# Projection stage of a two-layer attention kernel: where the squares and the normalising factors of q, k and v are computed

## Chip, cores and metric

The kernel runs on one core of a Trainium2 chip. The metric is the device time of one execution in microseconds, the median of several runs. The core has a matrix engine (TensorE, PE in the rows), a vector engine (VectorE, DVE), an activation engine (ScalarE, ACT), a general engine (GpSimd, POOL) and a queue engine (SyncE, SP). Each follows its own instruction list; they wait for one another only through semaphores.

## Reference

The part that the change touches is the front of the first layer's attention. With `hs` of 4 x 1024 tokens and 128 features, 16 heads of width 64:

```python
q = _silu(hs @ Wq + bq).reshape(Bn, Ln, H, DK).transpose(0, 2, 1, 3)
k = _silu(hs @ Wk + bk).reshape(Bn, Ln, H, DK).transpose(0, 2, 1, 3)
v = _silu(hs @ Wv + bv).reshape(Bn, Ln, H, DV).transpose(0, 2, 1, 3)
beta = jax.nn.sigmoid(hs @ Wb + bb).transpose(0, 2, 1)
...
q = q * jax.lax.rsqrt(jnp.sum(q * q, axis=-1, keepdims=True) + 1e-06)
k = k * jax.lax.rsqrt(jnp.sum(k * k, axis=-1, keepdims=True) + 1e-06)
...
g = (hs @ Wg + bg).reshape(Bn, Ln, H, DV)
```

The recurrence over tokens, a gated output projection, a quantised feed-forward block and a second layer (causal attention and eight experts) follow or precede; the change leaves them alone.

## The kernel before

The program is a row of phases. Each ends with `end_phase`, at which all five engines wait for one another, so nothing of the next phase starts before the slowest engine of this one is through. The change touches the projection phase alone.

In that phase the 4096 tokens are 32 tiles (`T`) of 128. For each tile TensorE fills eight PSUM banks of 512 columns (q, k, v and g, two banks each); a bank is one fp32 product (L1631, two recorded matmuls) and one bf16 product that adds the bias (L1632). Bank n of a tile waits for ACT's `Silu` of bank n of the tile before (`p_silu`). ACT turns the banks into `prj`, which holds four tiles (L1891), and waits before a tile until the store of the tile four earlier has landed (`p_stored`). GpSimd squares q, k and v, 1024 columns each, into `prj_sq`, which has one slot for each of the three (L1506); the slot must have been read by the reduction of the tile before (`p_red`). VectorE sums the squares by head (L2072) into `prj_n` for q and k and into `vv` for v. ACT takes the square root of the 32 sums of q and k (L1895). VectorE takes the reciprocal (L2077), copies the roots of beta, `sb_tok`, beside them as the factors of v (L2079), multiplies those of k by them (L2080), and scales the 3072 columns of q, k and v in place (L2082, `p_normed`). SP then stores the tile (L1379). VectorE does this with a lag of one tile: the three reductions of tile i, then the factors and the scaling of tile i-1. Each engine's order is the order in which the code is written; there is no scheduler.

After the last tile VectorE multiplies `vv` twice by `sb_tok` (L2084, L2085), TensorE turns it (L1637), ACT takes roots (L1899), SP stores them, and the phase ends. The next phase starts with loads of `ka` from the stored projections.

Of the kernel before, what the change touches and what calls it, by code (L numbers as in the profile page):

```python
# [10 lines left out]
ALU = mybir.AluOpType  # L11
ACT = mybir.ActivationFunctionType
AX = mybir.AxisListType.X
ds = bass.ds

P = 128
D = 128
B, L = 4, 1024
T = B * L // P
H0, DK = 16, 64  # L20
HD = H0 * DK
# [40 lines left out]
def layer_kernel(nc, a, out):  # L62

    ctx = ExitStack()
    with ctx:
        def sem(name):
            return ctx.enter_context(nc.semaphore(name))

        def sb(name, shape, dt=F32, scope=ctx):
            return scope.enter_context(nc.sbuf_tensor(name, shape, dt))  # L70
# [23 lines left out]
        bank = [banks[:, 512 * n:512 * n + 512] for n in range(8)]  # L94
# [35 lines left out]
        s2 = ExitStack()  # L130
# [8 lines left out]
        prj = sb("prj", [P, 4, 4 * HD], scope=s2)  # L139
        prj_sq = sb("prj_sq", [P, 3, HD], scope=s2)  # L140
        prj_n = sb("prj_n", [P, 2, 2, 2 * H0], scope=s2)
        prj_f = sb("prj_f", [P, 2, 3 * H0], scope=s2)
        prj_eps = sb("prj_eps", [P, 1], scope=s2)
        sbeta = sb("sbeta", [H0, B * L], scope=s2)
        sb_tok = sb("sb_tok", [P, T, H0], scope=s2)
        vv = sb("vv", [P, T, H0], scope=s2)
# [197 lines left out]
        p_sq = sem("p_sq")  # L344
        p_mm = sem("p_mm")
        p_silu = sem("p_silu")
        p_var = sem("p_var")
        p_std = sem("p_std")
        v_prj = sem("v_prj")
        p_normed = sem("p_normed")  # L350
        p_red = sem("p_red")
        p_stored = [sem(f"p_stored{n}") for n in range(2)] + [hq_done, h_turned]
        res_out, res_in = hT_done, down_done
        prj_sems = p_stored[2:4] + [res_out, res_in]
# [30 lines left out]
        sbt_set = sem("sbt_set")  # L385
# [67 lines left out]
        cleared = sem("cleared")  # L453
# [16 lines left out]
        def end_phase(eng):  # L470

            phases[eng] = phases.get(eng, 0) + 5
            eng.drain().then_inc(phase, 1)
            eng.wait_ge(phase, phases[eng])
# [79 lines left out]
        def prob_at(j):  # L554
            return sum(TB - x for x in range(j)) * P
# [927 lines left out]
        def _(pool):  # L1483
# [13 lines left out]

            for x in prj_sems:
                pool.sem_clear(x).then_inc(cleared, 1)
            for i in range(T):  # L1500
                for w in range(3):
                    pool.wait_ge(p_silu, 8 * i + 2 * w + 2)
                    if i:
                        pool.wait_ge(p_red, 3 * (i - 1) + w + 1)
                    x = prj[:, i % 4, HD * w:HD * w + HD]
                    pool.tensor_tensor(prj_sq[:, w, :], x, x, ALU.mult).then_inc(p_sq, 1)  # L1506
            end_phase(pool)
            chunk_pool(pool)
            with capped(pool):
# [321 lines left out]
        def _(act):  # L1831
# [50 lines left out]
            act.activation(sbeta[:, :], gates[0:H0, :], ACT.Sqrt).then_inc(sb_root, 1)  # L1882
            act.wait_ge(bias_set, 7)
            act.wait_ge(cleared, len(prj_sems))
            for i in range(T + 1):
                if i < T:
                    if i >= 4:
                        act.wait_ge(p_stored[i % 4], 16 * (i // 4))
                    for n in range(8):
                        act.wait_ge(p_mm, 8 * i + n + 1)  # L1890
                        act.activation(prj[:, i % 4, 512 * n:512 * n + 512], bank[n], ACT.Silu).then_inc(p_silu, 1)  # L1891
                if i >= 1:
                    y = (i - 1) % 2
                    act.wait_ge(p_red, 3 * (i - 1) + 2)
                    act.activation(prj_n[:, y, 1, :], prj_n[:, y, 0, :], ACT.Sqrt, bias=prj_eps[:, 0:1]).then_inc(p_std, 1)  # L1895
            act.wait_ge(g_stored, 16)
            for n in range(8):
                act.wait_ge(vv_turned, n + 1)
# [74 lines left out]
            for kind, s, k in program:  # L1973
                if kind == "b":
# [4 lines left out]
                    at, w = prob_at(j) + first - P * j, end - first  # L1979
# [14 lines left out]
        def _(dve):  # L1994
# [58 lines left out]
            bia = Count(dve, bias_set)  # L2053
            bia.n = 1
            bia.link(dve.memset(bias3[:, :], 0.0))
            bia.link(dve.memset(prj_eps[:, :], 1e-6))
            bia.link(dve.tensor_copy(bias_hi[:, :], raw3))
            bia.link(dve.scalar_tensor_tensor(out=rest3, in0=bias_hi[:, :], scalar=bias_part[:, 0:1], in1=raw3, op0=ALU.mult, op1=ALU.add))
            bia.link(dve.tensor_copy(bias_hi[:, :], rest3))
# [2 lines left out]
            dve.tensor_copy(sb_tok[:, :, :].rearrange("p t h -> p (t h)"), bank[0]).then_inc(sbt_set, 1)  # L2062
            dve.wait_ge(sbt_set, 1)
            prc = Count(dve, v_prj)
            for i in range(T + 1):
                if i < T:
                    y = i % 2
                    if i >= 2:
                        dve.wait_ge(p_std, i - 1)
                    for w, dst in ((0, prj_n[:, y, 0, 0:H0]), (1, prj_n[:, y, 0, H0:2 * H0]), (2, vv[:, i, :])):  # L2070
                        dve.wait_ge(p_sq, 3 * i + w + 1)
                        dve.tensor_reduce(dst, prj_sq[:, w, :].rearrange("p (h d) -> p h d", d=DK), AX, ALU.add).then_inc(p_red, 1)  # L2072
                if i >= 1:
                    t, y = i - 1, (i - 1) % 2
                    root = sb_tok[:, t, :]
                    dve.wait_ge(p_std, t + 1)
                    dve.reciprocal(prj_f[:, y, 0:2 * H0], prj_n[:, y, 1, :]).then_inc(v_prj, 1)  # L2077
                    prc.n += 1
                    prc.link(dve.tensor_copy(prj_f[:, y, 2 * H0:3 * H0], root))  # L2079
                    prc.link(dve.tensor_tensor(prj_f[:, y, H0:2 * H0], prj_f[:, y, H0:2 * H0], root, ALU.mult))  # L2080
                    qkv3 = prj[:, t % 4, 0:3 * HD].rearrange("p (h d) -> p h d", d=DK)
                    dve.tensor_tensor(qkv3, qkv3, prj_f[:, y, :].unsqueeze(2).to_broadcast([P, 3 * H0, DK]), ALU.mult).then_inc(p_normed, 1)  # L2082
            dve.wait_ge(p_red, 3 * T)
            prc.link(dve.tensor_tensor(vv[:, :, :], vv[:, :, :], sb_tok[:, :, :], ALU.mult))  # L2084
            dve.tensor_tensor(vv[:, :, :], vv[:, :, :], sb_tok[:, :, :], ALU.mult).then_inc(p_var, 1)  # L2085
# [2 lines left out]
            with capped(dve):  # L2088
# [11 lines left out]
                with dve.Fori(0, L // (2 * STEPS)) as i:  # L2100
# [3 lines left out]
                    for s in range(2 * STEPS):  # L2104
                        n, k = s // STEPS, s % STEPS
# [36 lines left out]
            for i in range(T + 3):  # L2142
                if i < T:
                    y = i % 2
# [5 lines left out]
                if 1 <= i <= T:  # L2150
                    j, y = i - 1, (i - 1) % 2
# [54 lines left out]
            y = 0  # L2206
            for step in (1, 2, 4, 8, 16):
                seq.link(dve.tensor_tensor(scan[:, 1 - y, PAD:PAD + T, :], scan[:, y, PAD:PAD + T, :], scan[:, y, PAD - step:PAD - step + T, :], ALU.add))
                y = 1 - y
# [6 lines left out]
            y = 0  # L2216
            for step in (1, 2, 4):
                seq.link(dve.tensor_tensor(escan[:, 1 - y, EP:EP + E1], escan[:, y, EP:EP + E1], escan[:, y, EP - step:EP - step + E1], ALU.add))
                y = 1 - y
# [54 lines left out]
            for kind, s, k in program:  # L2274
# [11 lines left out]
                elif kind == "t":  # L2286
# [3 lines left out]
                    b, p = s // 8, s % 8  # L2290
# [68 lines left out]
```

## Time and profile before

| what | us |
|---|---|
| median of 3 runs (3980.31 to 3981.28) | 3980.58 |
| the profiled execution, its own time | 4008.47 |
| its span | 4006.8 |
| first product of the projection phase starts | 409.25 |
| last VectorE instruction of the phase starts | 750.24 |

The times of single instructions below are those of the profiled execution, which took 27.89 us more than the median. Of the span VectorE is busy for 2816.8 us and TensorE for 3203.3 us, but that is a mean over phases with different limits: what the change is worth is to be read from the stretch from 409 to 751 us alone. In a group row the number after the bar is busy time and the mean duration of one in ns; in a row of the timeline the first number is the start and the second the time from the start of the first instruction to the end of the last of the `xN` that are merged. The bracket names idle time ahead of the instruction and what ended it.

### The profile page before, as it was taken

To read this page: it belongs to the slowest core of one execution; us is meant where nothing else is said; L and a number is where in the kernel's file an instruction comes from. 1 tells how busy PE (TensorE), PEld (TensorE's weight loads), DVE (VectorE), ACT (ScalarE), POOL (GpSimd) and SP (SyncE) were. 2 spreads that over 40 slices of the span, in tenths; PEclk is the share of its full clock that TensorE was granted. 3 is DMA by queue.
4 is the path that set the end of the run, shared out by engine and by line. 5 is a ranking of instruction groups with operands and counts; after the bars stand their busy time and mean duration, and the time that the engine had idled before them with its cause. 6 is when DMAs were issued, how large, how long until landed. Compare 5 with 4: busy or idle time off the path is not lost. (4 is left out here: it accounts for less than half of the span.)

```text
span 4006.8 us, 67365 instructions
## 1 busy us (share of the span) xinstructions
PE 3203.3 (80%) x24599; PEld 2425.8 (61%) x24695; DVE 2816.8 (70%) x4372; ACT 1583.7 (40%) x2709; POOL 1484.5 (37%) x1838
## 2 busy tenths in 40 slices
PE   0675988474189999999999999999946366899888
PEld 0343433364178888888988888899935263333334
DVE  8787799489347776676757777566668634777775
ACT  0222666353033333333333333333324243555554
POOL 0010555375145555455555555455545503000000
PEclk9996999777599999999999999999979687999999
DMA  1001244655512222322232132222246421111101
GB/s 26 0 0 35 126 210 202 204 115 127 163 35 53 51 54 57 71 51 53 57 71 53 35 73 57 64 43 47 55 164 193 139 69 33 25 22 19 25 17 30
DMA packets 433911, 293.12 MB, mean 73 GB/s; under 512 B 334891, under 2 KB 395883, under 8 KB 424813
## 3 DMA queue, kind: packets, MB, share of 16 engines
q1 hardware_dynamic: 418768, 263.98, 24.1%
q10 hardware_dynamic: 4608, 16.78, 1.4%
q0 software_dynamic: 10240, 8.41, 1.4%
q8 instruction: 188, 3.08, 0.4%
q14 instruction: 107, 0.88, 0.1%
HBM read 159.59 MB, written 129.45 MB: 72 GB/s over the span
## 5 line engine op out<-in xcount | busy, mean ns | idle before, releaser
L786 POOL TENSOR_TENSOR ssm<-ss_sb,lmask 128x512 f32<-128x512 f32 x384 | 506.9, 1334 | 493.7 <-issue 468.5
L2278 DVE TENSOR_REDUCE mx<-banks 128x2 f32<-128x1024 f32 (+3 forms) x384 | 360.8, 956 | 178.9 <-PE banks L1748 110.5
L1981 ACT ACTIVATE probs<-banks 128x1024 f32<-128x1024 f32 (+3 forms) x384 | 310.6, 811 | 303.3 <-PE banks L1770 155.9
L1053 ACT COPY xs<-banks 128x512 f32<-128x512 f32 x384 | 225.2, 587 | 388.1 <-PE banks L888 383.7
L900 PE MATMUL banks<-xs,ttw 128*128 128x128 f32 x2048 | 294.3, 287 | 11.5 <-ACT xs L1053 11.5
L793 POOL TENSOR_TENSOR ag<-ah,gt_sb 128x512 f32<-128x512 f32 x128 | 163.8, 1279 | 365.2 <-ACT ah L1078 365.2
L1631 PE MATMUL banks<-wproj,xnT 128*128 128x512 f32 x512 | 270.5, 610 | 30.5 <-ACT prj L1891 28.5
L1241 DVE TENSOR_TENSOR tw<-blk,banks 128x512 f32<-128x512 f32 x128 | 88.1, 688 | 270.8 <-PE banks L900 270.8
L888 PE MATMUL banks<-tw,ssm 128*128 128x128 f32 x2048 | 271.4, 276 | 0.0
L900 PEld LDWEIGHTS banks<-xs,ttw 128*128 128x128 f32 x2048 | 250.8, 193 | 30.3 <-ACT xs L1053 14.8
L1506 POOL TENSOR_TENSOR prj_sq<-prj 128x1024 f32<-128x1024 f32 x96 | 183.8, 1941 | 210.6 <-DVE prj_n L2072 121.9
L888 PEld LDWEIGHTS banks<-tw,ssm 128*128 128x128 f32 x2048 | 249.8, 192 | 0.0
L1241 DVE TENSOR_TENSOR tw<-tw,banks 128x512 f32<-128x512 f32 x256 | 176.1, 688 | 104.4 <-PE banks L900 104.4
L1768 PE MATMUL banks<-q_less,k_pad 128*128 128x512 bf16 (+3 forms) x737 | 198.2, 329 | 62.8 <-DVE mx L2278 48.9
L1059 ACT COPY ttw<-banks 128x512 f32<-128x512 f32 x256 | 151.1, 590 | 227.1 <-PE banks L907 227.1
L1748 PE MATMUL banks<-k_pad,q_parts 128*128 128x512 bf16 (+3 forms) x719 | 195.6, 330 | 22.7 <-issue 12.9
L1222 DVE TENSOR_TENSOR stk<-banks,umask 128x512 f32<-128x512 f32 x128 | 88.3, 690 | 168.0 <-ACT ss_sb L1044 167.2
L927 PE MATMUL banks<-stk,tw 128*128 128x192 f32 x1024 | 202.5, 342 | 0.8 <-DVE tw L1241 0.8
L1786 PE MATMUL banks<-probs,vaug 128*9 128x256 f32 (+3 forms) x1920 | 184.2, 424 | 0.0
L1631 PEld LDWEIGHTS banks<-wproj,xnT 128*128 128x128 f32 x512 | 97.8, 194 | 130.3 <-ACT prj L1891 76.7
L1748 PEld LDWEIGHTS banks<-k_pad,q_parts 128*128 128x128 bf16 x768 | 64.3, 98 | 179.6 <-issue 82.1
L728 POOL DMA_DIRECT2D nblk_s<-ssa x256 | 144.7, 565 | 73.9 <-ACT ssa L1016 52.1
(354 smaller groups left out, 7773.5 us busy)
## 6 DMA issues: line engine op xcount, KB each, us to landing
proj_s<-prj SPq DMA_DIRECT2D x32, 2048.0 KB, 6.3
qkv_t<-proj_s SPq DMA_DIRECT2D x32, 1536.0 KB, 7.8
ka<-proj_s ACTq DMA_DIRECT2D x32, 512.0 KB, 4.2
mem_s<-o_sb SPq DMA_DIRECT2D x32, 512.0 KB, 3.0
om<-mem_s SPq DMA_DIRECT2D x32, 512.0 KB, 3.9
om<-proj_s SPq DMA_DIRECT2D x32, 512.0 KB, 4.9
blk<-blk_s SPq DMA_DIRECT2D x256, 48.0 KB, 4.1
blk_s<-res SPq DMA_DIRECT2D x16, 512.0 KB, 4.7
```

The source lines that it names most:

```text
L786: pool.tensor_tensor(ssm[:, lv, :, :], ss_sb[:, k % 2, :, :], lmask[:, lv, :].unsqueeze(1).to_broadcast([P, 4, P]), ALU.mult).then_inc(mas ...
L888: last = pe.matmul(cols(bk[3], m), ssm[:, lv, m, :], inverse(tw, 0, k, lv, m, h), start=True, stop=True)
L900: last = pe.matmul(cols(bk[0], m), inverse(ttw, 1, k, lv, m, h), xs[:, k % 2, m, :], start=True, stop=True)
L927: last = pe.matmul(cols(bk[p], m % 2, P + DK), tw[:, k % 2, m, :], stk[:, k % 2, m, :], start=True, stop=True)
L1053: act.copy(xs[:, k % 2, :, :].rearrange("p h t -> p (h t)"), slot4(k)[3]).then_inc(x_set[lv], 1)
L1241: dve.tensor_tensor(tw[:, y, :, :], old, ps4(bk[0]), ALU.subtract).then_inc(tw_set[lv], 1)
L1631: pe.matmul(bank[n], xnT[:, P * i:P * i + P], wproj[:, 512 * n:512 * n + 512], start=True, stop=False)
L1748: last = pe.matmul(at[:, e, 0:w], q_parts[:, n, m, t * P:t * P + P], k_pad[:, n, e, m, 512 * c:512 * c + w], start=True, stop=(c != t // 4))
L1768: last = pe.matmul(at[:, e, 0:end - first], k_pad[:, n, e, m, P * j:P * j + P], q_less[:, s % 2, first:end], start=True, stop=(first != P ...
L1786: last = pe.matmul(bank[6][row:row + SLOT, n0 * P:512], vaug[:, b * TB + j, 2 * (s % 8) + e, :], p_, start=(j == 0), stop=(j == 6 + odd))
L1981: act.activation(probs[:, s % 2, :, at:at + w], slot_of((kind, s, k))[:, :, 0:w], ACT.Exp, scale=D1 ** -0.5).then_inc(b_read, 1)
L2278: dve.tensor_reduce(mx[:, s % 2, c, :, t:t + 1].rearrange("p e a -> p (e a)"), slot_of((kind, s, k))[:, :, 0:w], AX, ALU.max).then_inc(a_r ...
```

## The change

- The squares of q, k and v move from GpSimd to ACT, as `Square`, among the `Silu` of the same tile: after `Silu` 2, 4 and 6.
- ACT's square root and VectorE's reciprocal, copy and small product go. GpSimd computes the factors with three small instructions per tile: it adds 1e-6 to the 32 sums, raises them to the power -0.5 (a tensor of -0.5, `prj_pow`), and multiplies the sixteen of k by `sb_tok`.
- `prj_f` now has a slot for each of the 32 tiles, and the factors of v are filled in once ahead of the tiles by one VectorE copy of 128x512.
- VectorE does the reductions of q and k of tile i, the scaling of tile i-1, and then the reduction of v of tile i.

```diff
-        prj_f = sb("prj_f", [P, 2, 3 * H0], scope=s2)
-        prj_eps = sb("prj_eps", [P, 1], scope=s2)
+        prj_f = sb("prj_f", [P, T, 3 * H0], scope=s2)
+        prj_pow = sb("prj_pow", [P, 2 * H0], scope=s2)
...
-            for i in range(T):
-                for w in range(3):
-                    pool.wait_ge(p_silu, 8 * i + 2 * w + 2)
-                    if i:
-                        pool.wait_ge(p_red, 3 * (i - 1) + w + 1)
-                    x = prj[:, i % 4, HD * w:HD * w + HD]
-                    pool.tensor_tensor(prj_sq[:, w, :], x, x, ALU.mult).then_inc(p_sq, 1)
+            pool.wait_ge(sbt_set, 2)
+            for t in range(T):
+                sums = prj_n[:, t % 2, 0, :]
+                pool.wait_ge(p_red, 3 * t + 2)
+                pool.tensor_scalar(prj_n[:, t % 2, 1, :], sums, 1e-6, None, ALU.add).then_inc(p_std, 1)
+                pool.wait_ge(p_std, 3 * t + 1)
+                pool.tensor_tensor(prj_f[:, t, 0:2 * H0], prj_n[:, t % 2, 1, :], prj_pow[:, :], ALU.pow).then_inc(p_std, 1)
+                pool.wait_ge(p_std, 3 * t + 2)
+                pool.tensor_tensor(prj_f[:, t, H0:2 * H0], prj_f[:, t, H0:2 * H0], sb_tok[:, t, :], ALU.mult).then_inc(p_std, 1)
...
-            for i in range(T + 1):
-                if i < T:
-                    if i >= 4:
-                        act.wait_ge(p_stored[i % 4], 16 * (i // 4))
-                    for n in range(8):
-                        act.wait_ge(p_mm, 8 * i + n + 1)
-                        act.activation(prj[:, i % 4, 512 * n:512 * n + 512], bank[n], ACT.Silu).then_inc(p_silu, 1)
-                if i >= 1:
-                    y = (i - 1) % 2
-                    act.wait_ge(p_red, 3 * (i - 1) + 2)
-                    act.activation(prj_n[:, y, 1, :], prj_n[:, y, 0, :], ACT.Sqrt, bias=prj_eps[:, 0:1]).then_inc(p_std, 1)
+            for i in range(T):
+                if i >= 4:
+                    act.wait_ge(p_stored[i % 4], 16 * (i // 4))
+                for n in range(8):
+                    act.wait_ge(p_mm, 8 * i + n + 1)
+                    act.activation(prj[:, i % 4, 512 * n:512 * n + 512], bank[n], ACT.Silu).then_inc(p_silu, 1)
+                    if n in (2, 4, 6):
+                        w = n // 2 - 1
+                        act.wait_ge(p_silu, 8 * i + n)
+                        if i:
+                            act.wait_ge(p_red, 3 * (i - 1) + w + 1)
+                        act.activation(prj_sq[:, w, :], prj[:, i % 4, HD * w:HD * w + HD], ACT.Square).then_inc(p_sq, 1)
...
-            bia.link(dve.memset(prj_eps[:, :], 1e-6))
+            bia.link(dve.memset(prj_pow[:, :], -0.5))
...
+            dve.wait_ge(cleared, len(prj_sems))
+            dve.tensor_copy(prj_f[:, :, 2 * H0:3 * H0], sb_tok[:, :, :]).then_inc(sbt_set, 1)
             for i in range(T + 1):
                 if i < T:
-                    y = i % 2
-                    if i >= 2:
-                        dve.wait_ge(p_std, i - 1)
-                    for w, dst in ((0, prj_n[:, y, 0, 0:H0]), (1, prj_n[:, y, 0, H0:2 * H0]), (2, vv[:, i, :])):
+                    for w in range(2):
                         dve.wait_ge(p_sq, 3 * i + w + 1)
-                        dve.tensor_reduce(dst, prj_sq[:, w, :].rearrange("p (h d) -> p h d", d=DK), AX, ALU.add).then_inc(p_red, 1)
+                        dve.tensor_reduce(prj_n[:, i % 2, 0, H0 * w:H0 * w + H0], prj_sq[:, w, :].rearrange("p (h d) -> p h d", d=DK), AX, ALU.add).then_inc(p_red, 1)
                 if i >= 1:
-                    t, y = i - 1, (i - 1) % 2
-                    root = sb_tok[:, t, :]
-                    dve.wait_ge(p_std, t + 1)
-                    dve.reciprocal(prj_f[:, y, 0:2 * H0], prj_n[:, y, 1, :]).then_inc(v_prj, 1)
-                    prc.n += 1
-                    prc.link(dve.tensor_copy(prj_f[:, y, 2 * H0:3 * H0], root))
-                    prc.link(dve.tensor_tensor(prj_f[:, y, H0:2 * H0], prj_f[:, y, H0:2 * H0], root, ALU.mult))
+                    t = i - 1
+                    dve.wait_ge(p_std, 3 * t + 3)
                     qkv3 = prj[:, t % 4, 0:3 * HD].rearrange("p (h d) -> p h d", d=DK)
-                    dve.tensor_tensor(qkv3, qkv3, prj_f[:, y, :].unsqueeze(2).to_broadcast([P, 3 * H0, DK]), ALU.mult).then_inc(p_normed, 1)
+                    dve.tensor_tensor(qkv3, qkv3, prj_f[:, t, :].unsqueeze(2).to_broadcast([P, 3 * H0, DK]), ALU.mult).then_inc(p_normed, 1)
+                if i < T:
+                    dve.wait_ge(p_sq, 3 * i + 3)
+                    dve.tensor_reduce(vv[:, i, :], prj_sq[:, 2, :].rearrange("p (h d) -> p h d", d=DK), AX, ALU.add).then_inc(p_red, 1)
```

How this stands in the built programs, at two engines. The first piece is ACT at the start of the tiles in the kernel before: two tiles of `Silu`, the root of tile 0, then one tile and one root in turn.

```order
L1891 ACT_TABLE_LOAD [waits p_mm,cleared]
L1891 ACTIVATE prj<-banks 128x512 [waits bias_set]
L1891 ACTIVATE prj<-banks 128x512 [waits p_mm] x15
L1895 ACT_TABLE_LOAD
L1895 ACTIVATE prj_n<-prj_n,prj_eps 128x32 [waits p_red]
L1891 ACT_TABLE_LOAD
L1891 ACTIVATE prj<-banks 128x512 [waits p_mm] x8
```

The same place in the changed kernel, whose line numbers are its own (L1892 is the `Silu`, L1898 the `Square`):

```order
L1892 ACT_TABLE_LOAD [waits p_mm,cleared]
L1892 ACTIVATE prj<-banks 128x512 [waits bias_set]
L1892 ACTIVATE prj<-banks 128x512 [waits p_mm] x2
L1898 ACTIVATE prj_sq<-prj 128x1024 [waits p_silu]
L1892 ACTIVATE prj<-banks 128x512 [waits p_mm] x2
L1898 ACTIVATE prj_sq<-prj 128x1024 [waits p_silu]
L1892 ACTIVATE prj<-banks 128x512 [waits p_mm] x4
```

The roots and the two table loads of each tile are gone; three squares stand among the `Silu`, and no table load stands between a `Silu` and a `Square`. One load remains ahead of the roots after the last tile.

VectorE over one tile in the kernel before:

```order
L2072 TENSOR_REDUCE prj_n<-prj_sq 128x16 [waits p_sq,p_std]
L2072 TENSOR_REDUCE prj_n<-prj_sq 128x16 [waits p_sq]
L2072 TENSOR_REDUCE vv<-prj_sq 128x16 [waits p_sq]
L2077 RECIPROCAL prj_f<-prj_n 128x32 [waits p_std]
L2079 COPY prj_f<-sb_tok 128x16
L2080 TENSOR_TENSOR prj_f<-prj_f,sb_tok 128x16 [waits v_prj]
L2082 TENSOR_TENSOR prj<-prj,prj_f 128x3072 [waits v_prj]
```

and in the changed kernel:

```order
L2074 TENSOR_REDUCE prj_n<-prj_sq 128x16 [waits p_sq] x2
L2079 TENSOR_TENSOR prj<-prj,prj_f 128x3072 [waits p_std]
L2082 TENSOR_REDUCE vv<-prj_sq 128x16 [waits p_sq]
```

Seven instructions per tile have become four, and the reduction of v stands behind the scaling. GpSimd, in place of three 1024-column products per tile, has there

```order
L1504 TENSOR_SCALAR prj_n<-prj_n 128x32 [waits p_red]
L1506 TENSOR_TENSOR prj_f<-prj_n,prj_pow 128x32 [waits p_std]
L1508 TENSOR_TENSOR prj_f<-prj_f,sb_tok 128x16 [waits p_std]
```

each of which waits for the one ahead of it, and the first for the reduction of k of its tile.

## Rows read from the trace of the kernel before

**Rows 1.** Busy time by engine in the projection phase (view by stretches).

```profile
core 0: us, PE busy (x) PEld busy (x) DVE busy (x) ACT busy (x) POOL busy (x), PEclk, DMA share, GB/s
409.00:750.00 341.00, 286.75 (x752) 123.34 (x768) 318.89 (x226) 221.60 (x350) 183.77 (x96) 0.95 0.45 190
500.00:700.00 200.00, 173.61 (x458) 73.97 (x466) 198.70 (x137) 134.83 (x216) 107.81 (x58) 0.98 0.48 204
```

**Rows 2.** Timeline of VectorE over one tile, to the next scaling.

```profile
642.44 3.36 DVE L2082 TENSOR_TENSOR prj<-prj,prj_f 128x3072 f32<-128x3072 f32 x1
645.72 2.34 DVE L2072 TENSOR_REDUCE prj_n<-prj_sq 128x16 f32<-128x1024 f32 x2
647.97 1.21 DVE L2072 TENSOR_REDUCE vv<-prj_sq 128x16 f32<-128x1024 f32 x1
649.10 0.34 DVE L2077 RECIPROCAL prj_f<-prj_n 128x32 f32<-128x32 f32 x1
649.36 1.49 DVE L2079 COPY prj_f<-sb_tok 128x16 f32<-128x16 f32 x1
650.88 1.82 DVE L2080 TENSOR_TENSOR prj_f<-prj_f,sb_tok 128x16 f32<-128x16 f32 x1
652.73 3.36 DVE L2082 TENSOR_TENSOR prj<-prj,prj_f 128x3072 f32<-128x3072 f32 x1
```

**Rows 3.** Timelines of GpSimd and of ACT beside them.

```profile
647.07 5.60 POOL L1506 TENSOR_TENSOR prj_sq<-prj 128x1024 f32<-128x1024 f32 x3 [4.70 <-DVE prj_n L2072]
...
648.43 1.28 ACT L1891 ACT_TABLE_LOAD   x1
652.11 4.03 ACT L1891 ACTIVATE prj<-banks 128x512 f32<-128x512 f32 x8 [2.40 <-DMA proj_s<-prj]
656.15 1.28 ACT L1895 ACT_TABLE_LOAD   x1
```

**Rows 4.** Timeline of VectorE: the same small instructions with GpSimd idle.

```profile
442.88 0.11 DVE L2079 COPY prj_f<-sb_tok 128x16 f32<-128x16 f32 x1
443.02 0.18 DVE L2080 TENSOR_TENSOR prj_f<-prj_f,sb_tok 128x16 f32<-128x16 f32 x1
```

**Rows 5.** Timelines of PE: start of the phase, an unbroken stretch, a gap, the end.

```profile
409.25 2.05 PE L1631 MATMUL banks<-wproj,xnT 128*128 128x512 f32 x2 [0.94 <-DVE sb_tok L2062]
...
415.57 1.02 PE L1631 MATMUL banks<-wproj,xnT 128*128 128x512 f32 x2
...
420.94 1.02 PE L1631 MATMUL banks<-wproj,xnT 128*128 128x512 f32 x2
...
444.58 0.59 PE L1631 MATMUL banks<-wproj,xnT 128*128 128x512 f32 x1
...
652.76 1.12 PE L1631 MATMUL banks<-wproj,xnT 128*128 128x512 f32 x2 [1.37 <-ACT prj L1891]
...
751.07 6.38 PE L1637 MATMUL banks<-ident,vv 128*16 128x128 f32 x32 [25.49 <-DVE vv L2085]
```

**Rows 6.** Timeline of ACT: a `Silu` that waits for its bank, while PE is unbroken.

```profile
422.22 0.60 ACT L1891 ACTIVATE prj<-banks 128x512 f32<-128x512 f32 x1 [0.48 <-PE banks L1632]
```

**Rows 7.** Groups of ACT and GpSimd in other phases (nearest to the new instructions).

```profile
L1918 ACT ACTIVATE osq<-om 128x1024 f32<-128x1024 f32 x32 | 33.9, 1060 | 26.4 <-DMA om<-proj_s 26.4
...
L779 POOL TENSOR_SCALAR bx<-bt,rf_abs 128x12 f32<-128x12 f32 x256 | 81.7, 319 | 24.6
...
L776 POOL TENSOR_TENSOR bt<-bx,bd 128x24 f32<-128x24 f32 x128 | 50.9, 398 | 24.2 <-DMA bd<-vnorm_s 24.2
```

**Rows 8.** Timelines at the start of the second layer: GpSimd beside VectorE.

```profile
3105.69 4.50 POOL L1554 TENSOR_SCALAR_AFFINE_SELECT above<-above 128x128 bf16<-128x128 bf16 x1
3110.15 0.29 POOL L1554 TENSOR_SCALAR_AFFINE_SELECT below<-below 128x128 bf16<-128x128 bf16 x1
...
3105.61 4.42 DVE L487 TENSOR_TENSOR xnT<-xn 128x4096 f32<-128x4096 f32 x1
3110.07 4.42 DVE L488 TENSOR_REDUCE stats<-xnT 128x32 f32<-128x4096 f32 x1
```

**Rows 9.** DMA issues of the projection phase.

```profile
proj_s<-prj SPq DMA_DIRECT2D x24, 2048.0 KB, 6.3
```

**Rows 10.** Timelines of VectorE and ACT at the end of the phase.

```profile
749.52 0.68 DVE L2084 TENSOR_TENSOR vv<-vv,sb_tok 128x512 f32<-128x512 f32 x1
750.24 0.69 DVE L2085 TENSOR_TENSOR vv<-vv,sb_tok 128x512 f32<-128x512 f32 x1
...
752.18 0.59 ACT L1899 ACTIVATE gates<-banks 16x512 f32<-16x512 f32 x1 [11.13 <-PE banks L1637]
...
756.39 1.73 ACT L1899 ACTIVATE gates<-banks 16x512 f32<-16x512 f32 x3 [0.27 <-PE banks L1637]
```

## The prediction, made before the changed kernel ran

> **What bounds the kernel now.** The page says TensorE 80% and VectorE 70% busy over the whole span, but phases end at a barrier, so I read only the projection phase. The view by stretches shows VectorE busy for 198.70 of the 200 us from 500 to 700, TensorE for 173.61, ACT for 134.83 and GpSimd for 107.81 [rows 1]. VectorE's timeline then gives the period: one scaling starts at 642.44, the next at 652.73, which is 10.29 us per tile without a gap [rows 2]. The other engines wait: TensorE 1.37 us at a tile's start [rows 5], ACT 2.40 us for a store to free a slot, GpSimd 4.70 us for a reduction [rows 3]. So VectorE sets the pace.
>
> Its 10.29 us are the scaling 3.28 (642.44 to 645.72), the three reductions 3.38 (to 649.10), and 3.63 for reciprocal, copy and small product (to 652.73) [rows 2]. The last two are not work: the same copy and product take 0.11 and 0.18 us where GpSimd is idle [rows 4], and 1.49 and 1.82 us while GpSimd runs its triple square from 647.07 to 652.67 [rows 2, 3]. The two engines exclude each other there.
>
> What is next behind VectorE is TensorE. From 420.94 to 444.58 it works without a break, and 22 banks pass: 1.0745 us per bank, 8.60 us per tile of eight [rows 5]. The granted clock of the phase is 0.95 to 0.98, thus nearly all at 2.4 GHz, with slower products only behind gaps [rows 1]; with fewer gaps it should not be lower.
>
> **The change part by part.**
>
> VectorE loses 3.63 us per tile and keeps 3.28 + 3.38 = 6.66 us [rows 2]. Against TensorE's 8.60 it has 1.9 us to spare.
>
> GpSimd loses three squares, 5.60 us per tile [rows 3], which makes VectorE's stalls behind it impossible at that size.
>
> ACT loses two table loads of 1.28 us [rows 3] and the small root, and gains three squares of 1024 columns. The same operation on the same shape takes 1.06 us elsewhere in this kernel [rows 7]. A `Silu` that waits for its bank takes 0.60 us [rows 6]. The sum is 8 x 0.60 + 3 x 1.06 = 7.98 us per tile, under 8.60. The built order has no table load between `Silu` and `Square`, and each square needs the `Silu` before the one just issued, so no pipeline is waited out. I walk one tile, counted from the start z of its first bank on TensorE. A bank's `Silu` starts 1.28 us after the bank (420.94 to 422.22) [rows 5, 6], so `Silu` 2 ends at 2 x 1.0745 + 1.28 + 0.60 = 4.03. The square of q follows to about 5.05, that of k lies at 6.2 to 7.2, that of v at 8.4 to 9.4, and `Silu` 7 at 9.4 to 10.0, just as the next tile's first is ready. ACT keeps up with TensorE, which besides is up to eight banks ahead.
>
> VectorE then reduces q at 5.05 to 6.25 and k at 7.25 to 8.45, scales the tile before at 8.45 to 11.8 and reduces v to 13.0; the next q is ready at 13.65. Every slot of `prj_sq` is free in time: the latest, v, is read by 13.0 and written again from 17.0. The scaled tile is stored by z + 8.60 + 11.8 + 6.3 = z + 26.7 [rows 9], and ACT wants its slot at z + 34.4 + 1.3. So ACT's wait for a store goes too, even if the transfer grew by several us.
>
> GpSimd's new chain starts when k is reduced, at z + 8.45, as VectorE starts the scaling. Here a row decides who goes first: a GpSimd select on 128 columns took 4.50 us beside a VectorE product of two SBUF inputs that ran from 3105.61 to 3110.03, and the next one of its kind, beside a reduction, took 0.29 [rows 8]. So I let the chain wait until 11.8. The Trainium skill ("GPSIMD Engine Reference", Specifications) says that these engines share their SBUF interfaces and contend where VectorE reads two SBUF inputs; by that rule, the trace agrees with its 4.50. Were there no contention, the end of the phase would come 0.6 us earlier, no more.
>
> The chain is an addition, a power and a product. The addition and the product I take at 0.32 us each, from the small scalar operation [rows 7], and 0.1 us for each of two waits between. The power is in no row. From below I take the two-input product of 24 columns at 0.40 us, or less; from above 0.32 us for 12 columns, scaled to 32 as if all were paid per column: 0.85 us [rows 7]. Neither row is a power, which could be far slower, so I take the upper value, 0.85; the rest is a rival below. The chain is 0.32 + 0.1 + 0.85 + 0.1 + 0.32 = 1.7 us, from z + 11.8 to z + 13.5. Its result is wanted at z + 17.05, when the next k is reduced. So 3.5 us are to spare: a power of up to 4.4 us changes nothing in the pace. The added waits queue nothing: GpSimd has no other work in the phase. The Trainium skill (same page, Performance versus the Vector engine) gives about 12 cycles per element for branching bodies on this engine; as an estimate that page would make 32 columns at 1.2 GHz cost 0.32 us, and the end of the phase 0.5 us earlier than mine.
>
> The one copy ahead of the tiles (128x512, under 1 us) lies between 409 us and the first reduction, while TensorE starts. It costs nothing, since TensorE doesn't wait for it.
>
> At the end of the phase the load of the root's table, 1.28 us [rows 3], now stands behind the first turned bank. The eight roots went at TensorE's pace, with pauses of 0.27 us for some 0.59 of work [rows 10]; a late start is caught up but for about 0.3 us. Nothing else late: the last store lands 6.3 us after the scaling, before the roots are through.
>
> **The sum.** TensorE starts at 409.25 as before, and its third bank is done at 415.57, behind the slow first products. 253 banks remain: 253 x 1.0745 = 271.8, so the last bank is done at 687.4, and the last tile's z is 678.8. k of tile 31 is reduced at 687.3; the scaling of tile 30 runs to 690.6, v is reduced to 691.8, the chain ends at 690.6 + 1.7 = 692.3, the last scaling at 695.7, and two products of 0.7 each [rows 10] end at 697.1. Before, that point was 750.24 + 0.69 = 750.93. The gain is 53.8 us, less 0.3 for the table load: 53.5. What follows stands behind a barrier and moves as a whole. The profiled execution, 4008.47 us, would become 3955.0. It is slower than the median by 0.7%; the gain scaled the same way is 53.1, and 3980.58 - 53.1 = 3927.5.
>
> **Rivals.**
>
> *The power is slow and GpSimd sets the pace (slower).* If the chain and the scaling exclude each other [rows 8], a tile costs 3.36 + 0.32 + 0.1 + p + 0.1 + 0.32 = 4.2 + p, p being the power. At p = 4.4 this passes TensorE's 8.60. The phase before had (750.93 - 409.25) = 341.7 us; at 4.2 + p per tile for 31 tiles plus some 18 us at both ends it breaks even near p = 6.2, which is 194 ns per column. At p = 8 it costs 31 x (12.2 - 10.44) = 55 us: 4035 us. For it: no row shows this operation, and an engine that computes it in software could take such a time. Against it: every small GpSimd instruction shown takes 0.3 to 0.4 us [rows 7], and it would have to be fifteen times that. Chance 0.15.
>
> *A middling power, 4.4 to 6.2 us.* TensorE is not reached; halfway, at 5.3, the tile takes 9.5 us, the gain is 25 us and the time 3955. Chance 0.05.
>
> *ACT or VectorE comes out a little over TensorE.* If squares and `Silu` cost 9.0 us per tile with their waits, or the scaling must first wait for a running GpSimd instruction of each tile, a tile takes 0.4 us more, 13 us in all: 3940. For it: ACT's margin is only 0.6 us. Against it: back to back, eight `Silu` take 4.03 and not 4.80 [rows 3]. Chance 0.09.
>
> *Nothing changes, since something else holds the pace.* The store would have to: its 6.3 us to landing per 8.60 us tile [rows 9], and DMA busy for 0.48 of the time at 204 GB/s [rows 1], which would become 0.57. Chance 0.02; time 3980.
>
> **The numbers.** The forecast, a phase at TensorE's pace, has 0.69 and lies at 3924 to 3931, from the ends of the power's price below 4.4 us. With the case at 3940 it is 0.78, and to leave out no more than 0.2 the range reaches a little into the middling one: 3920 to 3948. Faster by over 0.2% (8 us, about what a measurement of this kernel can tell from no change) is 0.69 + 0.09 + 0.04 = 0.82; within it 0.03; slower 0.15.
>
> **What would show it.** Right: TensorE's products of the phase in one unbroken row at 1.07 us per bank and its last bank near 687; VectorE with some 1.9 us idle per tile, ended by ACT's squares; no ACT wait for the store; the last product of `vv` ending near 697; GpSimd's addition stretched to some 3.4 us beside the scaling. Wrong: VectorE's scaling waiting for GpSimd's product, or GpSimd's power at over 4 us. A power that long is what would make the prediction wrong by much; a `Square` of over 1.3 us would make it wrong by a little.

## The result, and the profile after

The changed kernel takes 3954.96 us (median of 4 runs, 3947.83 to 3958.68) against 3980.44 us: a ratio of 0.9934, 95% interval [0.9917, 0.9952]. It is 25.5 us faster; 53 us were forecast, and the range of 3920 to 3948 us missed it by 7 us.

The view by stretches answers to [rows 1]. Its columns are the same.

```profile
500.00:700.00 200.00, 190.07 (x520) 81.03 (x518) 141.80 (x86) 146.62 (x237) 194.68 (x66) 1.00 0.53 226
```

GpSimd, 107.81 us busy of 200 before, is now busy for 194.68; VectorE fell from 198.70 to 141.80. TensorE is at 190.07, not unbroken. The groups of the phase (line, engine, operation, tiles and shapes, count | busy, mean ns | idle ahead and what ended it) say which GpSimd instruction it is:

```profile
L1506 POOL TENSOR_TENSOR prj_f<-prj_n,prj_pow 128x32 f32<-128x32 f32 x32 | 174.6, 5457 | 2.7
...
L1504 POOL TENSOR_SCALAR prj_n<-prj_n 128x32 f32<-128x32 f32 x32 | 107.5, 3360 | 85.0 <-DVE prj_n L2074 82.5
L2079 DVE TENSOR_TENSOR prj<-prj,prj_f 128x3072 f32<-128x3072 f32 x32 | 107.4, 3358 | 80.8 <-POOL prj_f L1508 80.8
L1898 ACT ACTIVATE prj_sq<-prj 128x1024 f32<-128x1024 f32 x96 | 102.4, 1067 | 58.0 <-DVE vv L2082 58.0
```

The power takes 5.46 us for 32 columns, and VectorE's scaling waits for GpSimd's product 80.8 us in all. ACT in turn waits 58.0 us for the reduction of v, which stands behind the scaling. One tile on GpSimd and VectorE, where [rows 2, 3] stood:

```profile
568.16 0.22 POOL L1508 TENSOR_TENSOR prj_f<-prj_f,sb_tok 128x16 f32<-128x16 f32 x1
568.46 3.46 POOL L1504 TENSOR_SCALAR prj_n<-prj_n 128x32 f32<-128x32 f32 x1
572.01 5.46 POOL L1506 TENSOR_TENSOR prj_f<-prj_n,prj_pow 128x32 f32<-128x32 f32 x1
577.54 0.22 POOL L1508 TENSOR_TENSOR prj_f<-prj_f,sb_tok 128x16 f32<-128x16 f32 x1
...
568.41 3.36 DVE L2079 TENSOR_TENSOR prj<-prj,prj_f 128x3072 f32<-128x3072 f32 x1 [2.64 <-POOL prj_f L1508]
571.69 1.21 DVE L2082 TENSOR_REDUCE vv<-prj_sq 128x16 f32<-128x1024 f32 x1
572.82 2.33 DVE L2074 TENSOR_REDUCE prj_n<-prj_sq 128x16 f32<-128x1024 f32 x2
577.80 3.36 DVE L2079 TENSOR_TENSOR prj<-prj,prj_f 128x3072 f32<-128x3072 f32 x1 [2.65 <-POOL prj_f L1508]
```

This is a closed loop of 9.39 us (568.41 to 577.80): the scaling begins 0.05 us ahead of the addition, the addition is held until the scaling is done (3.46 us, where the first one of the phase, alone, took 0.33), then 5.46 us of power, 0.22 of product, and only then the next scaling. Before, a tile took 10.29.

At the end of the phase, where [rows 10] stood:

```profile
718.58 3.36 DVE L2079 TENSOR_TENSOR prj<-prj,prj_f 128x3072 f32<-128x3072 f32 x1 [4.90 <-POOL prj_f L1508]
...
722.57 0.69 DVE L2085 TENSOR_TENSOR vv<-vv,sb_tok 128x512 f32<-128x512 f32 x1
...
724.50 1.28 ACT L1902 ACT_TABLE_LOAD   x1 [18.57 <-PE banks L1639]
725.80 4.10 ACT L1902 ACTIVATE gates<-banks 16x512 f32<-16x512 f32 x8
```

The first product of the phase starts at 407.62, the last of `vv` ends at 723.26: 315.6 us against 341.7 before. The 26.0 us between them agree with the measured 25.5. The two profiled executions themselves lie 54.8 us apart (3953.71 and 4008.47): 1.6 us ahead of the phase, 26.0 in it and 27.1 behind it. The last part is not the change's doing: this execution of the kernel before was itself 28 us slower than the median of the others. There the chain of waits of the profile before has a wait of 29.59 us at 3326, in the second layer, and one of 13.69 at 3358, neither of which the profile after has. Their cause is open.

```profile
3326.05 29.59 another core or an unknown queue
```

### The profile page after: what moved, and what is told of

Read it like the earlier page. It is cut to its first block and busy times, and to the rows that moved or that the text cites. A ratio compares the mean times of both kernels' runs of the same rounds, so it can differ in the third digit from the quotient of the medians.

```text
span 3952.1 us, 67341 instructions
## 1 busy us (share of the span) xinstructions
PE 3205.6 (81%) x24695; PEld 2422.9 (61%) x24695; DVE 2713.1 (69%) x4277; ACT 1585.6 (40%) x2713; POOL 1584.2 (40%) x1838
## 5 line engine op out<-in xcount | busy, mean ns | idle before, releaser
L900 PEld LDWEIGHTS banks<-xs,ttw 128*128 128x128 f32 x2048 | 250.6, 193 | 30.3 <-ACT xs L1053 14.8
L1750 PE MATMUL banks<-k_pad,q_parts 128*128 128x512 bf16 (+3 forms) x768 | 205.8, 332 | 6.7 <-DVE mx L2278 3.3
L1506 POOL TENSOR_TENSOR prj_f<-prj_n,prj_pow 128x32 f32<-128x32 f32 x32 | 174.6, 5457 | 2.7
L1038 ACT COPY kqt<-banks 128x512 f32<-128x512 f32 x128 | 75.1, 587 | 243.5 <-PE banks L849 243.5
L927 PEld LDWEIGHTS banks<-stk,tw 128*128 128x128 f32 x1024 | 168.0, 194 | 5.7 <-DVE tw L1241 1.0
```

The source lines that it names most:

```text
L900: last = pe.matmul(cols(bk[0], m), inverse(ttw, 1, k, lv, m, h), xs[:, k % 2, m, :], start=True, stop=True)
L927: last = pe.matmul(cols(bk[p], m % 2, P + DK), tw[:, k % 2, m, :], stk[:, k % 2, m, :], start=True, stop=True)
L1750: last = pe.matmul(at[:, e, 0:w], q_parts[:, n, m, t * P:t * P + P], k_pad[:, n, e, m, 512 * c:512 * c + w], start=True, stop=(c != t // 4))
```

## The experiments

All vary the projection phase alone. E1 to E4 ran together, the kernel before beside them at 3978.93 us; E5 to E8 ran together on another chip, the kernel before beside them at 4007.78 us. So each is compared with the kernel before of its own group: as a difference of the two medians in us, and as the measured ratio with its interval. That ratio differs from the quotient of the two medians by up to 0.0008, which is 3 us (in E7 it says 0.9876, the medians 0.9882).

| run | what | us | less than before beside it | ratio, 95% interval | phase, us |
|---|---|---|---|---|---|
| E1 | power replaced by a product | 3928.87 | 50.1 | 0.9877 [0.9860, 0.9893] | 286.3 |
| E2 | power of 16 columns | 3926.36 | 52.6 | 0.9870 [0.9854, 0.9887] | 288.8 |
| E3 | scaling two tiles behind | 3932.77 | 46.2 | 0.9884 [0.9867, 0.9900] | 291.5 |
| E4 | addition left out | 3926.00 | 52.9 | 0.9875 [0.9859, 0.9892] | 291.5 |
| E5 | before, table filled ahead | 4002.30 | 5.5 | 0.9987 [0.9977, 0.9996] | 333.8 |
| E6 | squares on ACT, no power | 3996.75 | 11.0 | 0.9970 [0.9959, 0.9982] | 326.9 |
| E7 | addition on VectorE | 3960.61 | 47.2 | 0.9876 [0.9859, 0.9892] | 290.0 |
| E8 | changed kernel again | 3982.23 | 25.6 | 0.9929 [0.9912, 0.9945] | 315.3 |

The last column is from the start of the first product of the phase to the end of the last of `vv`, in the profiled execution of each run; the kernel before has 341.7 there and the changed kernel 315.6.

### E1: is the power all that stands between the phase and TensorE?

```diff
-                pool.tensor_tensor(prj_f[:, t, 0:2 * H0], prj_n[:, t % 2, 1, :], prj_pow[:, :], ALU.pow).then_inc(p_std, 1)
+                pool.tensor_tensor(prj_f[:, t, 0:2 * H0], prj_n[:, t % 2, 1, :], prj_pow[:, :], ALU.mult).then_inc(p_std, 1)
```

> The changed kernel with the power replaced by a product of the same operands; the factors of q and k are therefore wrong values, nothing else differs. Theory A (the 5.46 us power is all that keeps the phase from TensorE's pace): the instruction takes about 0.25 us, TensorE's products stand in one row at 8.60 us per tile, the last product of vv ends near 695 to 697, and the kernel takes 26 us less than the changed one, about 3928 us. Theory B (ACT's squares and VectorE's order hold the pace as well, so that the power hides a second limit): a tile takes 8.9 to 9.4 us and the kernel 3938 to 3955 us.

The timelines of GpSimd and VectorE:

```profile
565.08 3.33 POOL L1504 TENSOR_SCALAR prj_n<-prj_n 128x32 f32<-128x32 f32 x1 [4.63 <-DVE prj_n L2074]
568.49 0.25 POOL L1506 TENSOR_TENSOR prj_f<-prj_n,prj_pow 128x32 f32<-128x32 f32 x1
...
564.91 3.35 DVE L2079 TENSOR_TENSOR prj<-prj,prj_f 128x3072 f32<-128x3072 f32 x1
568.17 1.21 DVE L2082 TENSOR_REDUCE vv<-prj_sq 128x16 f32<-128x1024 f32 x1
570.22 1.22 DVE L2074 TENSOR_REDUCE prj_n<-prj_sq 128x16 f32<-128x1024 f32 x1 [0.83 <-ACT prj_sq L1898]
572.37 1.22 DVE L2074 TENSOR_REDUCE prj_n<-prj_sq 128x16 f32<-128x1024 f32 x1 [0.93 <-ACT prj_sq L1898]
573.50 3.35 DVE L2079 TENSOR_TENSOR prj<-prj,prj_f 128x3072 f32<-128x3072 f32 x1
```

8.59 us per tile, no scaling waits for GpSimd, VectorE's idle time is ended by ACT's squares, and the phase's last product ends at 694.29. That is Theory A: ACT's squares, VectorE's new order and the stores keep up with TensorE, and with the power made cheap the forecast comes out.

### E2: what the power costs

```diff
-                pool.tensor_tensor(prj_f[:, t, 0:2 * H0], prj_n[:, t % 2, 1, :], prj_pow[:, :], ALU.pow).then_inc(p_std, 1)
+                pool.tensor_tensor(prj_f[:, t, H0:2 * H0], prj_n[:, t % 2, 1, H0:2 * H0], prj_pow[:, H0:2 * H0], ALU.pow).then_inc(p_std, 1)
...
+            bia.link(dve.memset(prj_f[:, :, 0:H0], 1.0))
```

> The power is taken for the 16 columns of k alone; the 16 factors of q are left at 1, so q is not normalised. Theory A (the power is paid per column): it takes half of 5.46, 2.7 us, the chain is ready before the scaling asks for it, and the pace is TensorE's: about 3928 us. Theory B (it is paid per instruction): still near 5.4 us, and the time is that of the changed kernel, 3955 us.

The group of the power:

```profile
L1506 POOL TENSOR_TENSOR prj_f<-prj_n,prj_pow 128x16 f32<-128x16 f32 x32 | 93.8, 2931 | 2.7
```

2.93 us for 16 columns and 5.46 for 32: (5.46 - 2.93) / 16 = 0.158 us per column and 0.40 us besides. So it is paid per column but for 0.40 us, and at half its length it is hidden, both as Theory A said. The product of the same shape in E1 took 0.25 us.

### E3: does the power exclude the scaling?

```diff
-            for i in range(T + 1):
+            for i in range(T + 2):
                 if i < T:
+                    if i >= 2:
+                        dve.wait_ge(p_std, 3 * (i - 2) + 1)
...
-                if i >= 1:
-                    t = i - 1
+                if i >= 2:
+                    t = i - 2
                     dve.wait_ge(p_std, 3 * t + 3)
```

> The scaling runs two tiles behind the reductions in place of one, so that GpSimd need not be ready when the next tile's k is reduced; all operations as in the changed kernel. Theory A (GpSimd and the scaling exclude each other whole): chain and scaling still add up, 6.1 + 3.3 = 9.4 us per tile, and the time stays at 3955 us; the scaling would be stretched beside the power. Theory B (only the wait for the chain put them behind one another, and the power itself leaves VectorE alone): GpSimd's 6.1 to 6.3 us per tile hide under TensorE's 8.60, and the time is about 3928 us.

GpSimd and VectorE over one tile:

```profile
560.24 5.46 POOL L1506 TENSOR_TENSOR prj_f<-prj_n,prj_pow 128x32 f32<-128x32 f32 x1
565.77 2.59 POOL L1508 TENSOR_TENSOR prj_f<-prj_f,sb_tok 128x16 f32<-128x16 f32 x1
568.45 0.29 POOL L1504 TENSOR_SCALAR prj_n<-prj_n 128x32 f32<-128x32 f32 x1
...
564.94 3.35 DVE L2081 TENSOR_TENSOR prj<-prj,prj_f 128x3072 f32<-128x3072 f32 x1
568.20 1.21 DVE L2084 TENSOR_REDUCE vv<-prj_sq 128x16 f32<-128x1024 f32 x1
```

The scaling starts at 564.94, in the middle of a running power, and takes 3.35 us as ever; the power takes its 5.46. What is held is the product that GpSimd starts at 565.77, inside the scaling: until 568.36, when the scaling has ended. That is Theory B: the two work side by side once the power runs, and the pace is 8.59 us. Theory A, by which chain and scaling add up whole, is refuted. The phase is 5.2 us longer than that of E1 (291.5 against 286.3), and the time 3.9 us longer. The 5.2 us lie at the end of the phase, where one scaling more stands behind the last reduction and waits 1.94 us for the last chain. ACT also waited 3.5 us in all for stores, as a slot is now kept one tile longer, which doesn't show in the pace. The rest of the distance to E4, whose phase is as long and whose time is 6.8 us shorter, lies outside the phase and isn't explained.

### E4: where the hold falls

```diff
-                pool.tensor_scalar(prj_n[:, t % 2, 1, :], sums, 1e-6, None, ALU.add).then_inc(p_std, 1)
-                pool.wait_ge(p_std, 3 * t + 1)
-                pool.tensor_tensor(prj_f[:, t, 0:2 * H0], prj_n[:, t % 2, 1, :], prj_pow[:, :], ALU.pow).then_inc(p_std, 1)
...
+                pool.tensor_tensor(prj_f[:, t, 0:2 * H0], sums, prj_pow[:, :], ALU.pow).then_inc(p_std, 1)
```

> The addition of 1e-6 is left out and the power reads the sums themselves, so the chain has two instructions. Theory A (whatever stands first on GpSimd is held for the scaling's 3.3 us): the power shows as about 8.6 us (3.14 held and 5.46 of its own), a tile takes 9.0 us, and the time is about 3942 us. Theory B (the power needs the shared port only for a moment and works on beside the scaling): it shows as 5.5 to 6 us, and the pace is TensorE's, 3928 us.

GpSimd's timeline and VectorE's scalings:

```profile
566.87 8.47 POOL L1504 TENSOR_TENSOR prj_f<-prj_n,prj_pow 128x32 f32<-128x32 f32 x1 [2.73 <-DVE prj_n L2072]
575.42 0.22 POOL L1506 TENSOR_TENSOR prj_f<-prj_f,sb_tok 128x16 f32<-128x16 f32 x1
575.60 5.43 POOL L1504 TENSOR_TENSOR prj_f<-prj_n,prj_pow 128x32 f32<-128x32 f32 x1
...
566.71 3.35 DVE L2077 TENSOR_TENSOR prj<-prj,prj_f 128x3072 f32<-128x3072 f32 x1
...
575.68 3.39 DVE L2077 TENSOR_TENSOR prj<-prj,prj_f 128x3072 f32<-128x3072 f32 x1 [0.29 <-POOL prj_f L1506]
```

Neither theory holds as it stood. Where the power starts 0.16 us behind the scaling it is held for 3.04 us (8.47); where it starts 0.08 us ahead of it, it isn't held and doesn't hold (5.43 beside 3.39). The two cases alternate from tile to tile, on average GpSimd needs 7.2 us per tile, and TensorE's pace is kept. So for the power the hold is decided at its start: in E4 by 0.2 us of difference in when it starts.

### E5: one part of the change on the kernel before

```diff
+            prc.link(dve.tensor_copy(prj_f[:, :, 2 * H0:3 * H0], sb_tok[:, :, :]))
...
-                    prc.link(dve.tensor_copy(prj_f[:, y, 2 * H0:3 * H0], root))
```

(`prj_f` has a slot for each tile, and the small product waits for the reciprocal itself.)

> The kernel before with one part of the change alone: the factors of v are filled in ahead of the tiles, so VectorE's copy per tile goes. Theory A (copy and small product each wait for whichever of GpSimd's squares is running to end, and without the copy the product has only one such wait): VectorE's tile falls from 10.29 us by one wait, about 1.5 to 1.8 us, to 8.5 to 8.8 us, and the time is 3928 to 3938 us. Theory B (the product simply takes over the copy's wait, since VectorE must wait for the squares anyway): the product takes 3.3 us, the tile stays at 10.2 us, and the time is about 3978 us.

VectorE's timeline, against [rows 2], and GpSimd's squares:

```profile
569.63 0.34 DVE L2078 RECIPROCAL prj_f<-prj_n 128x32 f32<-128x32 f32 x1
570.00 1.37 DVE L2079 TENSOR_TENSOR prj_f<-prj_f,sb_tok 128x16 f32<-128x16 f32 x1
571.41 5.00 DVE L2081 TENSOR_TENSOR prj<-prj,prj_f 128x3072 f32<-128x3072 f32 x1
...
567.60 5.59 POOL L1506 TENSOR_TENSOR prj_sq<-prj 128x1024 f32<-128x1024 f32 x3 [4.49 <-ACT prj L1891]
```

A tile takes 10.08 us in place of 10.29. The product took over the copy's wait, and the scaling the product's: 5.00 us for what takes 3.36. The second wait moved on to the next instruction, not, as Theory B said, into the product; but its conclusion holds, since VectorE must get past the same squares. The gain is 5.5 us: filling the table alone is worth little as long as the squares stay on GpSimd.

### E6: the change without the power

```diff
-                pool.tensor_tensor(prj_f[:, t, 0:2 * H0], prj_n[:, t % 2, 1, :], prj_pow[:, :], ALU.pow).then_inc(p_std, 1)
...
+                if i >= 1:
+                    act.wait_ge(p_red, 3 * (i - 1) + 2)
+                    act.activation(prj_n[:, (i - 1) % 2, 1, :], prj_n[:, (i - 1) % 2, 0, :], ACT.Sqrt, bias=prj_eps[:, 0:1]).then_inc(p_std, 1)
...
+                    prc.link(dve.reciprocal(prj_f[:, t, 0:2 * H0], prj_n[:, t % 2, 1, :]))
+                    prc.link(dve.tensor_tensor(prj_f[:, t, H0:2 * H0], prj_f[:, t, H0:2 * H0], sb_tok[:, t, :], ALU.mult))
```

> The changed kernel without the power: squares on ACT, the table filled ahead, but the root on ACT and the reciprocal and small product on VectorE as in the kernel before; GpSimd idle in the phase. Theory A (ACT sets the pace: eight Silu back to back 4.03 us, three squares 2.9, two table loads and a root 2.9): 9.8 us per tile or a little more, and 3960 to 3968 us. Theory B (ACT's work hides under TensorE's 8.60 us because of the eight banks): about 3928 us.

```profile
566.84 0.64 ACT L1883 ACTIVATE prj<-banks 128x512 f32<-128x512 f32 x1
567.50 1.28 ACT L1892 ACT_TABLE_LOAD   x1
568.80 0.32 ACT L1892 ACTIVATE prj_n<-prj_n,prj_eps 128x32 f32<-128x32 f32 x1
569.14 1.28 ACT L1883 ACT_TABLE_LOAD   x1
...
577.28 1.28 ACT L1892 ACT_TABLE_LOAD   x1
```

ACT's timeline is without a gap, 9.78 us per tile (567.50 to 577.28), as Theory A said. The phase is 14.8 us shorter than before, the kernel 11.0. So squares on ACT need the root to leave ACT; the power, slow as it is, is the better of the two (25.6 us in E8 against 11.0).

### E7 and E8: a mended version, and the yardstick

```diff
-                pool.wait_ge(p_red, 3 * t + 2)
-                pool.tensor_scalar(prj_n[:, t % 2, 1, :], sums, 1e-6, None, ALU.add).then_inc(p_std, 1)
-                pool.wait_ge(p_std, 3 * t + 1)
+                pool.wait_ge(v_prj, t + 1)
...
+                    dve.wait_ge(p_red, 3 * i + 2)
+                    dve.tensor_scalar(prj_n[:, i % 2, 1, :], prj_n[:, i % 2, 0, :], 1e-6, None, ALU.add).then_inc(v_prj, 1)
```

> The changed kernel with the addition of 1e-6 on VectorE, behind the reduction of k, so GpSimd's chain is the power and the product; everything is computed. Theory A (the addition held for the scaling, 3.46 us, is what the chain can't afford; a running power and a scaling leave each other alone): VectorE has room for 0.1 us per tile, GpSimd's tile is 5.8 us plus at most one hold of 3.1 us at every other tile, the pace is TensorE's, 8.60 us, and the time 3925 to 3930 us. Theory B (5.46 us of power is too much wherever it starts): over 3940 us.

> The changed kernel once more, unedited, beside the others on the same chip. Both theories: 3948 to 3958 us, 9.39 us per tile. It is the yardstick for the runs beside it.

VectorE's and GpSimd's timelines of E7:

```profile
564.03 0.18 DVE L2073 TENSOR_SCALAR prj_n<-prj_n 128x32 f32<-128x32 f32 x1
564.13 3.35 DVE L2079 TENSOR_TENSOR prj<-prj,prj_f 128x3072 f32<-128x3072 f32 x1
...
564.29 8.47 POOL L1503 TENSOR_TENSOR prj_f<-prj_n,prj_pow 128x32 f32<-128x32 f32 x1 [2.74 <-DVE prj_n L2073]
572.84 0.22 POOL L1505 TENSOR_TENSOR prj_f<-prj_f,sb_tok 128x16 f32<-128x16 f32 x1
573.02 5.42 POOL L1503 TENSOR_TENSOR prj_f<-prj_n,prj_pow 128x32 f32<-128x32 f32 x1
```

The addition costs VectorE 0.10 us of a tile in which it was idle for 1.76 (E1), GpSimd's alternation is that of E4, and the phase takes 290.0 us. E7 is 47.2 us faster than the kernel before and 21.6 us faster than the changed kernel beside it (E8, 3982.23), and no run of the one reaches the times of the other (at most 3962.10, at least 3978.62). The pace is Theory A's. The absolute times of E5 to E8 are not those that were expected, because this chip took 4007.78 us for the kernel before, 28.85 us more than the other. The difference lies behind the phase: from the phase's end to the end of the span the profiles of E5 to E8 take 3259 to 3262 us, those of E1 to E3 3229 to 3231. In E8's chain of waits stands the wait that the profile of before showed,

```profile
3305.10 29.69 another core or an unknown queue
```

again in the second layer. E5, E6 and E7 have shorter ones there, of 15.6 to 18.4 us, and the same time behind the phase to 3 us, so their comparison with one another stands. The cause is open. E7 computes everything that the kernel before does.

## Why the prediction was wrong

**The step that failed** is the price of the power. The prediction took it as 0.85 us, "the upper value" from 0.32 us for 12 columns scaled to 32. It measured 5.46 us (E2: 0.40 + 0.158 per column). The chain was put at 1.7 us from the end of the hold and is 5.46 + 0.22 + 0.2 = 5.9 us; with the hold it fills GpSimd for 9.39 us per tile. That row bounds a multiplication, and nothing in it bounds another operation: calling it the value from above was the error, and the range inherited it. A sentence beside it drew an estimate of 0.32 us from the Trainium skill ("GPSIMD Engine Reference", Performance versus the Vector engine; about 12 cycles per element for branching bodies); the measured 0.158 us per column is sixteen times the 0.01 us which that makes, so the rule doesn't cover this operation.

The price alone doesn't make the slow tile, though. The hold of the addition was in the prediction, at its right size of some 3.4 us; beside a cheap power it does no harm (E1), and E7, which has the same power but the addition on VectorE, takes 8.60 us per tile. It takes the dear power and the held addition together.

**The rival that came true** is the middling power of 4.4 to 6.2 us, "halfway, at 5.3, the tile takes 9.5 us, the gain is 25 us and the time 3955". Measured: 5.46 us, 9.39 us, 25.5 us, 3954.96 us. It had a chance of 0.05, and with the slow one beside it 0.20, for an operation that no row showed; the rows at hand could not make it so small. That its time is met to 0.04 us is partly luck: it was worked out for a power of 5.3 us and a tile of 9.5.

**Its formula** was 4.2 + p, thus 9.66 us at p = 5.46, and 9.39 came out. It put scaling and addition one behind the other, 3.36 + 0.32; in the trace the held addition is through at 571.92, only 0.15 us behind the scaling's end, and the product takes 0.22 us and not 0.32. The idea under it, that the chain and the scaling exclude each other, was only partly right: E3 and E4 show that a power once started goes on beside the scaling.

**What stood.** VectorE's remaining 6.66 us per tile: in E1 it is idle for 1.76 us of 8.59, ended by ACT, so 6.83 us remain. `Square` at 1.06 us: 1.067 measured in the changed kernel; in E1 ACT keeps TensorE's pace. The addition stretched to "some 3.4 us": 3.46. No wait of ACT for a store. The banks at 1.0745 us without a gap: E1's 8.59 per tile, and its phase of 286.3 us against the 287.9 (409.25 to 697.1) of the sum. The forecast of 3927.5 us is what the change gives without its slow power: 3928.87.

**Two small terms.** The 0.3 us for the late table load didn't show: from the last product of `vv` to the last root it was 7.2 us before [rows 10] and is 6.6 us (723.26 to 729.90). And the gain was scaled down by 0.7% because the profiled execution was slower than the median; the phase itself wasn't slower, as its 26.0 us against the measured 25.5 show, so there was nothing to scale.

## What to carry to other kernels

An operation that no row shows has no upper bound from rows of other operations, even on the same engine and shape; compute the value at which it becomes the bound and give the far side its full chance. On an engine with a long instruction, look at what is queued ahead of it: a tiny instruction of 0.3 us that starts inside another engine's long one cost 3.1 us of the chain, and moving it to an engine with idle time brought 21.6 us (E8 to E7), where the changed kernel had missed the forecast by 27.6. A wait taken away from one instruction may only move to the next (E5), so remove what is waited for.

## What the runs showed of the hardware

- GpSimd's power to -0.5 takes 5.46 us for 32 columns of 128 partitions and 2.93 for 16, thus 0.158 us per column and 0.40 us besides, if the cost is linear (no third length was run). All 32 powers of the changed kernel lie within 0.02 us of one another. A product of the same 32 columns takes 0.25 us.
- A GpSimd instruction that starts while VectorE runs a product of two SBUF inputs waited for its end in the cases shown: 3.46 for 0.33 us (addition), 2.59 for 0.22 (product), 8.47 for 5.43 (power). The Trainium skill ("GPSIMD Engine Reference", Specifications) names this contention; these numbers agree.
- The other way round it depends on the instruction. A running GpSimd power doesn't hold a VectorE product: 3.35 us beside it (E3) as alone. A running GpSimd square of 1024 columns holds VectorE's next such product to its end: 5.00 for 3.36 us (E5). The two differ in their columns, 32 and 1024, as well as in the operation, and which of them decides wasn't separated. That the power has read its inputs early and then only computes would explain it, but was not tested.
- VectorE's reductions of 1024 columns are not held: 1.21 us beside a running GpSimd square [rows 2, 3] and beside a running power.
- `Square` needs no table load between `Silu` (E1 to E4), and takes 1.05 us for 1024 columns in E1 and 1.07 in the changed kernel.
